# Paged attention of a twelve-sublayer decoder kernel: projections and attention in one program, stacks loaded between the stores, page rows brought by DMA

## The chip, the cores and the metric

The kernel runs on one core of one Trainium2 chip. The metric is the time of one execution on the device, in microseconds (us). The core has five engines that run their own instruction streams and wait for each other by semaphores: TensorE (PE, with its weight loads PEld), VectorE (DVE), ScalarE (ACT), GpSimd (POOL) and SyncE (SP), which issues nearly all DMA transfers of this kernel.

## The reference

The program is a decoder of four layers with three sublayers each (self attention, cross attention, feed-forward), every one wrapped as `x = layernorm(x + f(x))`, on `x` of 2 x 1024 x 256 in fp32. The change concerns the fourth sublayer, the self attention of layer 1. The rest of the reference is left out.

```python
def _L1_attn_ref(x, wq, w_down, wk_up, wv_up, wo):   # N_HEAD = 16, PAGE_SIZE = 64, x: 2 x 1024 x 256
    ...
    q = (x @ wq).reshape(B, T, H, D)
    lat = x @ w_down
    k = (lat @ wk_up).reshape(B, T, H, D)
    v = (lat @ wv_up).reshape(B, T, H, D)
    q = _apply_rope(q, cos, sin)
    k = _apply_rope(k, cos, sin)
    scores = jnp.einsum('bqhd,bkhd->bhqk', q, k) * scale
    pages = jnp.arange(T) // PAGE_SIZE
    allowed = pages[None, :] <= pages[:, None]
    scores = jnp.where(allowed[None, None], scores, jnp.finfo(scores.dtype).min)
    attn = jax.nn.softmax(scores, axis=-1)
    out = jnp.einsum('bhqk,bkhd->bqhd', attn, v).reshape(B, T, E)
    return out @ wo
```

## The kernel before

Every sublayer is a function ("stage") with one or more blocks; in a block each engine has its own program. At the end of each `Mem` its semaphores are cleared and all engines meet at a barrier. In the names of the profile and of the instruction lists the digit of the layer is left out, so `L1_attn_Q` is `L_attn_Q`.

`paged_attention_stage` has two blocks with such a barrier between them.

*The first block* (`L1_attn_qkv`, L186 to L304) makes q, k and v of both batches, in a loop that each engine runs twice (`Fori`). TensorE writes the projections into two PSUM tiles `Y`; VectorE applies the rotary factors (`full`, `rot`, L286 to L292); ScalarE and GpSimd split each result into three bf16 parts whose sum is the fp32 value (`parts`, L261, L300, L263, L303); SP stores the parts to HBM (`parts_dram`, L211). There are four such results in a batch (q in two halves, k in two halves), eight in all; they are called items 0 to 7 here. Each is stored by two transfers. `parts` has two buffers, so the first cast of an item (L261) waits for the stores of the item two before it. At the end SP waits for all stores. The weights and the rotary tables of this block lie in `L_attn_room`, loaded in an earlier stage.

*The second block* (`L1_attn`, from L307) is the attention, in eight rounds of four heads (`it`). For each round SP loads a stack Q and a stack K (`load`, L358 to L363): the parts from HBM, six to a stack and 16 partition rows each, so that one bf16 matmul over the stacked rows gives the product of the fp32 values. Three slots hold the stacks of three rounds. Above the 96 rows of the parts a stack has 8 page rows, which put the mask into the product; above those Q has three rows that SP writes for each round with the negated row maxima (the *neg rows*, L387, three transfers), and K has three rows of ones. A round has a first pass (`row_max`, L407, into `R`; VectorE takes the maxima, L530) and a second pass (scores, L453, into `S`; ScalarE exponentiates, L496; TensorE multiplies by v, L440, into `O`). The first pass of round 0 and twelve of the units of round 1 stand ahead of the second pass of round 0; later, the first pass runs ahead between the second pass's steps. The maxima are split into three bf16 parts on VectorE, turned on TensorE (L415, into `T`), copied by ScalarE (L487) and sent as neg rows; the scores of round 0 wait for them (`neg_in`).

Before the first pass can start, this block sets its constants on VectorE: a memset of `neg`, the ones rows of K in three slots (L518), the identity in bf16 (L519), and from two fp32 tiles `page_q` and `page_k`, which SP loads, the page rows of Q and of K in three slots (L523, L524). TensorE waits for all eleven (`const_set`). SP's order in this block is: output weights `wout`, the 13 transfers for the next sublayer (`following.load`, into `yT`), the page tiles, then the stacks of rounds 0, 1 and 2, and after that the neg rows as the maxima come.

## Time and profile before

| | us |
|---|---|
| runs | 2941.55, 2937.02, 2941.30 |
| median | 2941.3 |
| the profiled execution, its own time | 2937.35 |
| its span, first to last instruction | 2935.5 |
| the stage of the change in it, about | 553 to 960 |

The profile shows one execution. Its times are counted from the start of the span. What lies between the span and the execution's own time is 1.85 us. Busy shares of the whole span average over twelve different stages, so the sections below read the stage itself. "TensorE clock" is the granted clock as a share of 2.4 GHz: 0.50 is 1.2 GHz.

### The profile page before, as it was taken

The page shows a single profiled execution, that of the slowest core. Times are in us where ns is not written, and L with a number is a line of the kernel's source. Part 1 is how long each engine was busy: PE and PEld are TensorE (multiplying, and loading weights), DVE is VectorE, ACT ScalarE, POOL GpSimd, SP SyncE. Part 2 cuts the span into 40 slices and gives each one's busy share as a digit, 9 for nine tenths or more (in the row PEclk, how much of TensorE's full clock was granted, in tenths as well). Part 3 has the DMA queues.
Part 4 walks back from the last instruction along what each step waited for, and adds up shares of the span by engine and source line. Part 5 has one row for each costly group of instructions (what it writes and reads, how often), then busy time and mean ns, then how long its engine had stood idle before and what let it go on. Part 6 is the DMA issues. An engine that isn't in the chain of part 4 may idle for free. (4 is left out here: it accounts for less than half of the span.)

```text
span 2935.5 us, 35285 instructions
## 1 busy us (share of the span) xinstructions
PE 2414.5 (82%) x13995; PEld 1669.9 (57%) x14003; DVE 1503.2 (51%) x2550; ACT 857.4 (29%) x1223; POOL 488.7 (17%) x395
## 2 busy tenths in 40 slices
PE   5876756747888968975999998937999599999888
PEld 3665643422222767763666666735777467777674
DVE  8996966448775340014564565462111345545543
ACT  1111656412556212213433233201111222212132
POOL 3332320130000012311001000102221120000010
PEclk8898978966999979997999999857999799999979
DMA  3002000052441024532322221013222110000000
GB/s 106 0 1 100 2 30 1 11 130 44 67 70 30 13 75 179 212 135 88 92 64 89 61 65 58 8 56 97 96 97 87 68 52 17 17 12 17 1 31 29
DMA packets 71009, 176.71 MB, mean 60 GB/s; under 512 B 16478, under 2 KB 36447, under 8 KB 67280
## 3 DMA queue, kind: packets, MB, share of 16 engines
q1 hardware_dynamic: 60480, 122.60, 15.0%
q0 software_dynamic: 8208, 50.01, 4.8%
q8 instruction: 100, 1.64, 0.2%
q10 hardware_dynamic: 2176, 2.10, 0.2%
q14 instruction: 45, 0.37, 0.0%
HBM read 149.04 MB, written 25.43 MB: 59 GB/s over the span
## 5 line engine op out<-in xcount | busy, mean ns | idle before, releaser
L1575 PE MATMUL L_ffn_h_ps<-L_ffn_xgT,L_ffn_w 128*128 128x512 f32 (+2 forms) x992 | 241.7, 402 | 19.2 <-DMA L_ffn_w<-in_L_ffn_w,group_rows 16.9
L2215 PE MATMUL L_attn_X<-xT,L_attn_w 128*128 128x512 f32 x512 | 227.4, 597 | 0.0
L1587 PE MATMUL L_ffn_y_ps<-L_ffn_w,L_ffn_h 128*128 128x256 f32 x1008 | 223.0, 381 | 4.0 <-ACT L_ffn_h L1612 3.9
L1575 PEld LDWEIGHTS L_ffn_h_ps<-L_ffn_xgT,L_ffn_w 128*128 128x128 f32 x992 | 160.6, 199 | 101.2 <-issue 65.8
L530 DVE TENSOR_REDUCE L_attn_neg<-L_attn_R 128x1 f32<-128x512 f32 (+3 forms) x304 | 187.5, 658 | 54.8 <-PE L_attn_R L407 53.3
L1612 ACT ACTIVATE L_ffn_h<-L_ffn_h_ps,L_ffn_w 128x640 f32<-128x640 f32 (+2 forms) x184 | 101.5, 552 | 388.9 <-PE L_ffn_h_ps L1575 359.1
L1587 PEld LDWEIGHTS L_ffn_y_ps<-L_ffn_w,L_ffn_h 128*128 128x128 f32 x1008 | 190.2, 191 | 32.2 <-ACT L_ffn_h L1612 7.9
L407 PE MATMUL L_attn_R<-L_attn_K,L_attn_Q 104*128 104x512 bf16 (+3 forms) x384 | 119.7, 364 | 83.1 <-DVE L_attn_K L524 48.5
L496 ACT ACTIVATE L_attn_probs<-L_attn_S 128x1024 f32<-128x1024 f32 (+1 forms) x192 | 147.3, 812 | 79.5 <-PE L_attn_S L453 78.9
L2215 PEld LDWEIGHTS L_attn_X<-xT,L_attn_w 128*128 128x128 f32 x512 | 95.2, 191 | 110.1 <-issue 108.3
L1633 DVE COPY L_ffn_xgT<-L_ffn_t_ps 128x256 f32<-128x256 f32 x63 | 24.6, 421 | 246.9 <-PE L_ffn_t_ps L1562 246.9
L1642 DVE TENSOR_TENSOR L_ffn_yg<-L_ffn_y_ps,L_ffn_w 128x256 f32<-128x256 f32 x63 | 26.8, 425 | 227.5 <-PE L_ffn_y_ps L1587 227.5
L2511 PE MATMUL L_attn_X<-xT,L_attn_w 128*128 128x512 f32 x256 | 118.0, 606 | 9.5 <-DMA L_attn_w<-in_L_attn_w 8.9
L407 PEld LDWEIGHTS L_attn_R<-L_attn_K,L_attn_Q 104*128 104x128 bf16 x384 | 33.8, 100 | 157.1 <-DVE L_attn_neg L530 95.2
L1683 POOL DMA_INDIRECT token_outputs<-L_ffn_yg,puts x63 | 61.8, 981 | 366.1 <-DVE L_ffn_yg L1642 366.1
L453 PE MATMUL L_attn_S<-L_attn_Q,L_attn_K 107*128 107x512 bf16 (+3 forms) x384 | 96.3, 337 | 2.0 <-ACT L_attn_probs L496 1.9
L847 POOL TENSOR_TENSOR L_attn_v_all<-L_attn_q,L_attn_kv 128x2048 f32<-128x2048 f32 x16 | 73.9, 4623 | 140.4 <-DVE L_attn_q L780 124.5
L2736 POOL TENSOR_TENSOR L_attn_prod<-L_attn_k_sum,L_attn_qs 128x1024 f32<-128x1024 f32 x16 | 37.7, 2355 | 348.6 <-DVE L_attn_qs L2708 348.6
L2414 POOL TENSOR_TENSOR L_attn_sq_sum<-L_attn_sq_sum,L_attn_sq 128x1024 f32<-128x1024 f32 x14 | 33.0, 2359 | 347.1 <-ACT L_attn_sq L2305 347.1
L2295 ACT ACTIVATE L_attn_bc<-L_attn_bc 128x1024 f32<-128x1024 f32 x32 | 33.8, 1057 | 194.2 <-DVE L_attn_bc L2368 194.2
L440 PE MATMUL L_attn_O<-L_attn_probs,L_attn_v_all 128*32 128x512 f32 (+3 forms) x768 | 82.0, 505 | 0.0
L2511 PEld LDWEIGHTS L_attn_X<-xT,L_attn_w 128*128 128x128 f32 x256 | 48.6, 195 | 58.7 <-issue 57.3
(529 smaller groups left out, 4795.7 us busy)
## 6 DMA issues: line engine op xcount, KB each, us to landing
L_ffn_w<-in_L_ffn_w SPq DMA_DIRECT2D x8, 2180.0 KB
L_attn_bc<-decays SPq DMA_DIRECT2D x32, 512.0 KB, 6.5
L_attn_w<-in_L_attn_w SPq DMA_DIRECT2D x16, 640.0 KB, 3.9
L_attn_bp<-decays SPq DMA_DIRECT2D x32, 256.0 KB, 7.0
L_attn_Q<-L_attn_q_parts SPq DMA_DIRECT2D x48, 128.0 KB, 4.9
L_attn_K<-L_attn_k_parts SPq DMA_DIRECT2D x48, 128.0 KB, 7.4
L_attn_w<-in_L_attn_w SPq DMA_DIRECT2D x16, 384.0 KB, 3.1
token_outputs<-zero SPq DMA_DIRECT2D x1, 4096.0 KB, 20.7
```

Of the source, the lines that this page charges most:

```text
L407: mm = nc.tensor.matmul(R[n % 2][:, u * wdt:(u + 1) * wdt], Q[0:KM, par, j0 + u, tt * P:(tt + 1) * P], K[0:KM, par, j0 + u, c * CW:c * CW ...
L440: mm = nc.tensor.matmul(O[32 * j:32 * j + 32, lo:CW], v_all[:, it, gt, 32 * j:32 * j + 32], probs[:, (2 * n + j // 2) % 4, j % 2, lo:CW], ...
L453: mm = nc.tensor.matmul(S[e % 2][:, j % 2, lo:CW], K[0:KS, par, j, gt * P:(gt + 1) * P], Q[0:KS, par, j, tc * CW + lo:(tc + 1) * CW], star ...
L496: nc.scalar.activation(probs[:, e % 4, :, lo:CW], S[e % 2][:, :, lo:CW], ACT.Exp, scale=SCALE).then_inc(exp_done, 1)
L530: nc.vector.tensor_reduce(neg[:, c, j0:j0 + heads, tt], R[n % 2][:, 0:heads * width(tt, c)].rearrange("p (h k) -> p h k", h=heads), X_AXIS ...
L847: nc.gpsimd.tensor_tensor(prod[n % 2][:, h, :, :], q[n % 2][:, h, :].unsqueeze(2).broadcast_to([P, HALF, H, DH]), keys(n).unsqueeze(1).bro ...
L1575: ins = nc.tensor.matmul(h_ps[f % 2][:, lo // CW, 0:hi - lo], w1[u][:, kt, f * P:(f + 1) * P], xgT[u][:, kt, lo:hi], start=kt == 0, stop=k ...
L1587: ins = nc.tensor.matmul(y_ps[k % 2][:], h[:, f, t * P:(t + 1) * P], w2[u][:, f, :], start=f == 0, stop=f == FT - 1)
L1612: nc.scalar.activation(h[:, f, 0:n], h_ps[f % 2][:].rearrange("p c n -> p (c n)")[:, 0:n], func, bias=b1[g % 2][:, f:f + 1]).then_inc(sem[ ...
L1683: nc.gpsimd.indirect_dma_start(core.outputs, at, yg[g % 2][:, t, :], None).then_inc(y_stored[g % 2], 16)
L2215: ins = nc.tensor.matmul(x[:, c * CW:(c + 1) * CW], w[1 - par][:, kt, r, :], xT[:, kt, b * T + c * CW:b * T + (c + 1) * CW], start=kt == 0 ...
L2511: ins = nc.tensor.matmul(x[:, c * CW:(c + 1) * CW], w[o][:, kt, r, :], xT[:, kt, b * T + c * CW:b * T + (c + 1) * CW], start=kt == 0, stop ...
```

## The change

The two blocks become one, and the barrier between them is gone. Each engine runs its projection program and then, in the same block, its attention program. The loops over the batch are written out. Buffers are shared so that both parts fit: `full`, `rot`, `rest` and `latT` lie in `oT`, `probs` lies in `room` (which holds the projection weights and rotary tables), and `S`, `R`, `O` and `T` are parts of the two PSUM tiles `Y`. New waits keep them apart: TensorE's first maxima wait for `rot_done` of item 6 and for v, its first scores for `rot_done` of item 7, and ScalarE's first copy into `oT` for the last part of item 7.

The page rows and the rows of ones come as bf16 pairs packed into 32-bit words, made on the host and sent by six DMA transfers straight into the stacks, at the very start of the stage. The memsets and casts of VectorE are gone.

SP loads the stacks of rounds 0, 1 and 2 between the stores of the second batch; `wout` and the transfers for the next sublayer follow after the last store. Only loads from round 3 on wait for all stores.

The diff, cut to its core and without the pure re-indentation:

```diff
+    def load(sp, it):
+        par = it % SLOTS
+        for stack, which in ((Q, 0), (K, 1)):
+            for n, part in enumerate(PARTS[which]):
+                src = parts_dram[which][part:part + 1, it:it + 1, :, :].rearrange("c i (j d) t -> (c i d) j t", d=DH)
+                sp.dma_start(stack[n * DH:(n + 1) * DH, par, :, :], src).then_inc(stack_loaded[par], 16)
+
+    oT = m.sb("oT", [P, NI, T])
+    full, rot, rest, latT = oT[:, 0:2, :], oT[:, 2:4, :], oT[:, 4:6, :], oT[:, 6, :]
...
+    def projections_on_sync(sp):
+        for par in range(SLOTS):
+            for stack, rows, src in ((Q, slice(KP, KM), "page_q"), (K, slice(KP, KS), "page_k")):
+                sp.dma_start(stack[rows, par, :, :].rearrange("p j t -> p (j t)").bitcast(I32), A[src]).then_inc(pages_loaded, 16)
+        for b in range(B):
-                with sp.Fori(0, B) as b:
             for r in range(NR):
                 sp.wait_ge(part_done[2], b * NR + r + 1)
                 for g in range(2):
...
+                if b == 1 and r < SLOTS:
+                    sp.wait_ge(stored[r // 2], 16 * NR)
+                    load(sp, r)
-                for par in range(2):
-                    sp.wait_ge(stored[par], 16 * B * NR)
...
-            probs = m.sb("probs", [P, 4, 2, CW])
+        probs = room[:].rearrange("p (u j n) -> p u j n", u=4, j=2)
...
+        S = [Y[1][:, n, :, :] for n in range(2)]
+        R = [Y[0][:, 0, n, :] for n in range(2)]
+        O, Tp = Y[0][:, 1, 0, :], Y[0][:, 1, 1, 0:P]
...
         @block.sync
         def _(sp):
+            projections_on_sync(sp)
             sp.dma_start(wout[:], A[f"{name}_wout"]).then_inc(static_loaded, 16)
             following.load(sp)
-                sp.dma_start(page_q[KP:KM, :], A["page_q"]).then_inc(static_loaded, 16)
-                sp.dma_start(page_k[KP:KM, :], A["page_k"]).then_inc(static_loaded, 16)
...
-                for it in range(SLOTS):
-                    load(it)
...
                         sp.wait_ge(scores_mm, it * NE)
+                        for par in range(2):
+                            sp.wait_ge(stored[par], 16 * B * NR)
+                        load(sp, it + SLOTS - 1)
...
         @block.tensor
         def _(pe):
-                pe.wait_ge(static_loaded, 48)
-                pe.wait_ge(const_set, 11)
+            projections_on_tensor(pe)
+            pe.wait_ge(pages_loaded, 16 * 2 * SLOTS)
+            pe.wait_ge(rot_done, B * NR - 1)
+            pe.wait_ge(v_copied, B)
...
                 pe.wait_ge(neg_in, it * 48 + 48)
+                if it == 0:
+                    pe.wait_ge(rot_done, B * NR)
...
         @block.vector
         def _(dve):
+            projections_on_vector(dve)
             nc.vector.memset(neg[:], 3.0e38).then_inc(const_set, 1)
-                for par in range(SLOTS):
-                    nc.vector.memset(K[KP:KS, par, :, :], 1.0).then_inc(const_set, 1)
             nc.vector.tensor_copy(identb[:], core.ident[:]).then_inc(const_set, 1)
-                dve.wait_ge(static_loaded, 48)
-                dve.wait_ge(const_set, 5)
-                for par in range(SLOTS):
-                    nc.vector.tensor_copy(Q[KP:KM, par, :, :], over(page_q[KP:KM, :], G)).then_inc(const_set, 1)
-                    nc.vector.tensor_copy(K[KP:KM, par, :, :], over(page_k[KP:KM, :], G)).then_inc(const_set, 1)
-                dve.wait_ge(const_set, 11)
+            dve.wait_ge(const_set, 2)
```

How the instructions stand on the two engines that matter most, first on SP. Before, SP's last entries ahead of the neg rows (`L_attn_Q<-L_attn_negT`; the x6 is of rounds 0 and 1) are the end of the transfers for the next sublayer, the page tiles and the stacks of rounds 0 to 2:

```order
L2869 DMA yT<-in_L_xattn_hwf 128x512
L2869 DMA yT<-in_L_xattn_ob 128x256
L355 DMA L_attn_page_q<-in_page_q 8x1024
L356 DMA L_attn_page_k<-in_page_k 8x1024
L363 DMA L_attn_Q<-L_attn_q_parts 16x4x1024 x6
L363 DMA L_attn_K<-L_attn_k_parts 16x4x1024 x6
L363 DMA L_attn_Q<-L_attn_q_parts 16x4x1024 x6
L363 DMA L_attn_K<-L_attn_k_parts 16x4x1024 x6
L363 DMA L_attn_Q<-L_attn_q_parts 16x4x1024 x6
L363 DMA L_attn_K<-L_attn_k_parts 16x4x1024 x6
L387 DMA L_attn_Q<-L_attn_negT 1x32x128 x6
```

In the changed kernel the same stacks stand on SP between the stores of items 4, 5, 6 and 7 (rows with `_parts<-L_attn_parts`), and `wout` follows:

```order
L223 DMA L_attn_q_parts<-L_attn_parts 64x3x1024 x2
L198 DMA L_attn_Q<-L_attn_q_parts 16x4x1024 x6
L198 DMA L_attn_K<-L_attn_k_parts 16x4x1024 x6
L223 DMA L_attn_q_parts<-L_attn_parts 64x3x1024 x2
L198 DMA L_attn_Q<-L_attn_q_parts 16x4x1024 x6
L198 DMA L_attn_K<-L_attn_k_parts 16x4x1024 x6
L223 DMA L_attn_k_parts<-L_attn_parts 64x3x1024 x2
L198 DMA L_attn_Q<-L_attn_q_parts 16x4x1024 x6
L198 DMA L_attn_K<-L_attn_k_parts 16x4x1024 x6
L223 DMA L_attn_k_parts<-L_attn_parts 64x3x1024 x2
L353 DMA L_attn_wout<-in_L_attn_wout 128x1024
```

Behind `wout` come the 13 transfers of the next sublayer, of which these are the last, and then the neg rows:

```order
L2864 DMA yT<-in_L_xattn_ow 128x512
L2864 DMA yT<-in_L_xattn_hwf 128x512
L2864 DMA yT<-in_L_xattn_ob 128x256
L376 DMA L_attn_Q<-L_attn_negT 1x32x128 x6
L198 DMA L_attn_Q<-L_attn_q_parts 16x4x1024 x6
L198 DMA L_attn_K<-L_attn_k_parts 16x4x1024 x6
```

So the transfers of the next sublayer have moved from in front of the stacks to between the stacks and the neg rows.

On VectorE, before, between the end of the projection loop and the first reduction:

```order
L279 COMPARE_AND_BRANCH
L53 UNCONDITIONAL_BRANCH
L514 UNCONDITIONAL_BRANCH
L516 MEMSET L_attn_neg 128x64
L518 MEMSET L_attn_K 11x4096 x3
L519 CAST L_attn_identb<-ident 128x128
L523 CAST L_attn_Q<-L_attn_page_q 8x4096
L524 CAST L_attn_K<-L_attn_page_k 8x4096
L523 CAST L_attn_Q<-L_attn_page_q 8x4096
L524 CAST L_attn_K<-L_attn_page_k 8x4096
L523 CAST L_attn_Q<-L_attn_page_q 8x4096
L524 CAST L_attn_K<-L_attn_page_k 8x4096
```

In the changed kernel, from the rotary work of item 7 to the first reductions (`L_attn_Y` is now the PSUM tile of `R`):

```order
L296 TENSOR_TENSOR L_attn_oT<-L_attn_Y,L_attn_room 128x1024
L298 TENSOR_TENSOR L_attn_oT<-L_attn_Y,L_attn_room 128x1024
L302 TENSOR_TENSOR L_attn_oT<-L_attn_oT 128x1024
L517 MEMSET L_attn_neg 128x64
L518 CAST L_attn_identb<-ident 128x128
L524 TENSOR_REDUCE L_attn_neg<-L_attn_Y 128x4
```

Two of the eleven constants are left on VectorE, and no branch or barrier stands between the two programs.

## Rows read from the trace of the kernel before

**Rows 1.** The page: the span, and part 1, busy time of each engine.
```profile
span 2935.5 us, 35285 instructions
PE 2414.5 (82%) x13995; PEld 1669.9 (57%) x14003; DVE 1503.2 (51%) x2550; ACT 857.4 (29%) x1223; POOL 488.7 (17%) x395
```

**Rows 2.** Windows: busy us of PE, PEld, DVE, ACT, POOL; clock, DMA share, GB/s.
```profile
553.00:642.20 89.20, 59.91 (x144) 28.98 (x144) 30.02 (x24) 22.89 (x27) 34.72 (x16) 0.83 0.29 71
642.20:669.10 26.90, 0.00 (x0) 0.00 (x1) 24.07 (x11) 0.00 (x0) 0.00 (x0) 0.50 1.00 207
669.10:703.30 34.20, 28.41 (x66) 6.25 (x67) 32.04 (x54) 1.54 (x2) 0.00 (x0) 0.50 0.29 48
703.30:960.00 256.70, 223.73 (x1463) 72.54 (x1461) 176.62 (x298) 154.88 (x213) 16.55 (x7) 0.98 0.29 48
```

**Rows 3.** Timeline, 613 to 636 us: start, length, instruction, idle before it.
```profile
613.57 7.03 PE L231 MATMUL L_attn_qkv_Y<-L_attn_qkv_latT,L_attn_room 128*128 128x512 f32 x16
618.51 1.22 DVE L288 TENSOR_TENSOR L_attn_qkv_rot<-L_attn_qkv_Y,L_attn_room 128x1024 f32<-128x1024 f32 x1
626.58 1.23 DVE L292 TENSOR_TENSOR L_attn_qkv_full<-L_attn_qkv_full,L_attn_qkv_rot 128x1024 f32<-128x1024 f32 x1
627.26 2.52 POOL L303 TENSOR_TENSOR L_attn_qkv_parts<-L_attn_qkv_rest,L_attn_qkv_parts 128x1024 bf16<-128x1024 f32 x1 [1.16 <-ACT L_attn_qkv_parts L263]
629.49 1.04 ACT L261 CAST L_attn_qkv_parts<-L_attn_qkv_full 128x1024 bf16<-128x1024 f32 x1 [2.31 <-DMA L_attn_q_parts<-L_attn_qkv_parts]
633.89 2.12 POOL L303 TENSOR_TENSOR L_attn_qkv_parts<-L_attn_qkv_rest,L_attn_qkv_parts 128x1024 bf16<-128x1024 f32 x1 [1.15 <-ACT L_attn_qkv_parts L263]
```

**Rows 4.** Timeline, 642 to 670 us, VectorE and TensorE.
```profile
642.30 0.11 DVE L516 MEMSET L_attn_neg<- 128x64 f32 x1 [14.50 <-PEq L56]
669.13 1.01 PE L407 MATMUL L_attn_R<-L_attn_K,L_attn_Q 104*128 104x128 bf16 x6 [48.53 <-DVE L_attn_K L524]
669.82 25.54 DVE L530 TENSOR_REDUCE L_attn_neg<-L_attn_R 128x4 f32<-128x512 f32 x38 [0.80 <-PE L_attn_R L407]
```

**Rows 5.** Timeline of the DMA queue of SP, 615 to 666 us.
```profile
615.65 9.94 SPq L211 DMA_DIRECT2D L_attn_q_parts<-L_attn_qkv_parts  x4
649.49 2.67 SPq L363 DMA_DIRECT2D L_attn_Q<-L_attn_q_parts  x6
663.44 2.77 SPq L363 DMA_DIRECT2D L_attn_K<-L_attn_k_parts  x6
```

**Rows 6.** The instructions on stack K, 640 to 700 us.
```profile
L363 SPq DMA_DIRECT2D L_attn_K<-L_attn_k_parts x18: 425/426/428, 652.2 to 665.8; - x18
DMA to landing us min/median/max: 6.0/10.1/14.5
```

**Rows 7.** DMA issues, first stack, then third: KB each, median to landing.
```profile
L_attn_K<-L_attn_k_parts SPq DMA_DIRECT2D x6, 128.0 KB, 6.7
L_attn_K<-L_attn_k_parts SPq DMA_DIRECT2D x6, 128.0 KB, 13.5
```

**Rows 8.** Windows: stores of item 4, following weights, three stacks, a later stack.
```profile
616.90:620.40 3.50, 3.50 (x9) 1.33 (x7) 3.40 (x4) 1.04 (x1) 1.79 (x1) 1.00 0.89 221
643.10:651.90 8.80, 0.00 (x0) 0.00 (x0) 6.97 (x3) 0.00 (x0) 0.00 (x0) 0.50 0.96 288
651.90:679.10 27.20, 8.40 (x20) 1.93 (x20) 25.84 (x22) 0.00 (x0) 0.00 (x0) 0.50 1.04 170
771.30:781.80 10.50, 9.45 (x75) 3.56 (x76) 8.32 (x14) 5.71 (x9) 0.00 (x0) 1.00 1.02 142
```

**Rows 9.** Timeline, 699 to 703 us: the neg rows, the first scores.
```profile
699.46 1.89 SPq L387 DMA_DIRECT2D L_attn_Q<-L_attn_negT  x3
703.33 1.06 PE L453 MATMUL L_attn_S<-L_attn_Q,L_attn_K 107*128 107x512 bf16 x2
```

**Rows 10.** Timeline, 759 to 762 us: a cast on VectorE beside GpSimd.
```profile
759.32 2.36 POOL L586 TENSOR_TENSOR L_attn_oT<-L_attn_oT,L_attn_rden 128x1024 f32<-128x1024 f32 x1 [123.31 <-DMA L_attn_rden<-L_attn_inv_dram]
759.34 2.37 DVE L541 CAST L_attn_neg_parts<-L_attn_neg 128x32 bf16<-128x32 f32 x1
```

More of the change, by code:

```diff
@@ L181, in paged_attention_stage @@
     inv_dram = nc.dram_tensor(f"{name}_inv_dram", (G, T), F32, kind="Internal").ap()
[L182 removed]
+    v_all, weights, room, early = early
+    SLOTS = 3
+    PER = 16 * 2 * len(PARTS[0])
     wq = early.tiles["wq"].rearrange("p k (r d) -> p k r d", r=2)
     wk, wv, wdown, cos, sin = [early.tiles[n] for n in ("wk", "wv", "wdown", "cos", "sin")]
[L185 to L591 removed]
@@ L3396, in host_arrays, with halves @@
     own = np.arange(TT)[:, None] == t // P
-    a["page_q"] = np.where(own & (t % P < 64), -1.0e18, 0.0).astype(f)
-    a["page_k"] = np.where(own & (t % P >= 64), 1.0, 0.0).astype(f)
+    def halves(rows):
+        u = np.tile(rows.astype(f), (1, 4)).view(np.uint32)
+        u = (u + 0x7FFF + (u >> 16 & 1)) >> 16
+        return np.ascontiguousarray(u[:, 0::2] | u[:, 1::2] << 16).view(np.int32)
+    a["page_q"] = halves(np.where(own & (t % P < 64), -1.0e18, 0.0))
+    a["page_k"] = halves(np.concatenate([np.where(own & (t % P >= 64), 1.0, 0.0), np.ones((3, T))]))
     d = np.arange(DH)
```

663 lines of the change are left out of this document (320 added, 343 removed).

## The prediction

> **What bounds the kernel now.** The page [rows 1] says only that TensorE is busy for 82% of the span. That is an average over twelve sublayers, and the edit touches one of them, so I went to the windows of that sublayer [rows 2]. The second window is the find: from 642.2 to 669.1 us TensorE runs nothing, VectorE is busy for 24.07 of the 26.9 us with 11 instructions, and the DMA engines are full (share 1.00). Next I read the timeline on both sides of the hole. The last projection matmul starts its run at 613.57 and ends at 620.6; the split of the last part ends on GpSimd at 636.0; VectorE's first instruction of the attention program starts at 642.30 [rows 3, 4]. The first maxima matmul starts at 669.13, and it waited for VectorE's cast of the page rows (L524), 48.5 us of idle in all [rows 4]. So the path through this stage is: projections, last split, barrier at 642.2, eleven constants on VectorE, first maxima. From there VectorE's reductions set the pace (38 of them in 25.54 us without a gap) until the neg rows go out at 699.46 and the scores start at 703.33 [rows 4, 9].
>
> **What is removed.** The barrier with its wait for the last stores: 642.3 - 636.0 = 6.3 us [rows 3, 4]. The three memsets and six casts: nearly all of the 24.07 us that VectorE works before 669.1 [rows 2]. And the order: work that begins after the last split can now begin when its own inputs are there. Unrolling the projection loops changes none of the waits inside them, and I cost it at nothing: before them TensorE's matmuls follow one another without a gap (the run from 613.57 is 7.03 us for 16 [rows 3]), which hides whatever the loop's branches cost or the straight-line code costs to fetch.
>
> **When the first maxima matmul can start now.** It has three conditions; the latest counts.
> First, VectorE's `rot` of item 6: 618.51 + 1.22 = 619.7 [rows 3].
> Second, VectorE itself, which must be free to reduce. Its last projection add ends at 627.8 [rows 3]; then come the memset of neg and the cast of the identity. A cast can be held up by GpSimd: at 759.34 one took 2.37 us and ended together with a GpSimd tensor_tensor that had begun beside it [rows 10]. Here GpSimd works from 627.26 to 629.78 [rows 3], so I put VectorE free at 630.0.
> Third, stack 0. SP issues it after the two stores of item 4 (615.65 [rows 5]). Those stores fill the DMA engines until 620.4 [rows 8]. Behind them stand twelve transfers. In the trace, three stacks take 27.2 us at 170 GB/s with the engines full, so one takes 9.1 us, and the last semaphore comes at 665.8 + 14.5 = 680.3, 1.2 us behind the end of the data at 679.1 [rows 6, 8]. So stack 0 is in at 620.4 + 9.1 + 1.2 = 630.7, and issue doesn't bound it: all 36 issues took from 649.49 to 666.2 [rows 5], 5.6 us for each twelve.
> The stack is last by 0.7 us. The first maxima matmul starts at 630.8 instead of 669.1: **38.3 us** earlier. The cover of VectorE's preparation is thus thin, but being exposed would cost tenths.
>
> **What is late next.** Maxima and reductions take as long as before, since VectorE's reductions set their pace and not TensorE's clock, which is 0.50 in that window now too [rows 2]. So the neg rows are ready 699.46 - 669.13 = 30.3 us after the start, at 661.1. Undisturbed, scores follow 703.33 - 699.46 = 3.9 us later [rows 9], at 665.0. But the three neg transfers are issued on SP, behind everything that SP has issued, and that list has moved too: before, it had emptied by 679.1, twenty microseconds ahead of them [rows 8, 9]. Now, from 620.4 on, the engines have to move, in order of issue: stack 0, stores, stack 1, stores, stack 2, stores, and then the output weights with the thirteen transfers of the next sublayer. That is 3 x 9.1 for stacks, 3 x 3.5 for stores, and 8.8 for the weights [rows 8]: 46.6 us, to 667.0. I checked that the list never runs dry: SP has each next item out before the one ahead of it is done. The last stores depend on a split that now waits for the stores of item 5 queued behind stack 0 (in at about 634.2); it then needs the same 6.5 us as from 629.49 to 636.01 [rows 3], so they go out at 640.7, still ahead of the end of stack 1 at 642.1. The weights follow by 648. The neg rows, issued at 661.1, stand behind them all: data at 667.0, semaphore 1.2 later, scores at about **668.2**. Against 703.33 that is 35.1 us earlier; 3.2 of the 38.3 are handed back.
>
> That a transfer waits for those ahead of it is what the trace shows: the median time to landing of a K transfer grows from 6.7 us in the first stack to 13.5 us in the third, as the backlog grows [rows 7]. The Trainium skill says the same of the mechanism (DMA: Bandwidth & Descriptors, "Queues, rings and completion order"): on each DMA engine the descriptors of one issuing queue are consumed in ring order. By that page the sum is 35.1 us; if small transfers could pass, it would be 38.3 us.
>
> Nothing else is late. Stack 1 is wanted 26 us after the first maxima, at 657, and is in at 643. The page rows go out at the start of the stage, about 60 us ahead of their use. TensorE's wait for `rot` of item 7 and ScalarE's for the last part are over long before the scores start. Behind the delayed split nothing stands but the last stores. The remaining window (703.3 to 960, [rows 2]) holds the same instructions in the same order and moves as a whole, and so do all later sublayers, which start at barriers.
>
> **Sum.** The profiled execution took 2937.35 us (span 2935.5); minus 35.1 gives 2902.3. It lies 3.95 under the median of the three runs, 2941.3, so the forecast on that scale is 2941.3 - 35.1 = **2906.2**.
>
> **Rivals.**
> A, *the neg rows are not held up* (they pass, or the list empties sooner because stores and loads overlap better than one at a time). For it: a store alone reaches 221 GB/s and the weights 288 [rows 8], so mixing may help. Against: the share is already 0.89 to 1.04. It gives the full 38.3: 2903.0, and at most a microsecond more if stack 0 comes sooner, since VectorE is free at 630.0.
> B, *the stacks load slowly.* A later stack, with ScalarE and TensorE at work, went at 142 GB/s, 10.5 us and more [rows 8]; the three (27.2 us at 170 GB/s are 4.62 MB) then take 32.5 us. The list ends at 672.2, the scores start at 673.5, and the gain is 29.8: 2911.5. For it: other engines are now active beside the loads. Against: half the three-stack window had VectorE and TensorE at work and didn't slow.
> C, *the other side: the list in front of the neg rows outlasts the old start.* The place is the same wait. It decides once the list ends past 702.1: after stores and weights (19.3 us) that leaves 62.4 us for the 4.62 MB of stacks, 74 GB/s. At 60 GB/s they take 77.0 us, scores start at 718.0, and the time is 2956.0. Against: the lowest rate in any of these windows is 142.
> D, *nothing is gained*, because the start of the stack loads or of the maxima still hangs on the last store. The order of instructions speaks against it: SP issues stack 0 behind item 4's stores, and only loads from stack 3 on wait for all stores.
>
> **How the numbers follow.** My case (gain 33 to 37) has 0.52, A 0.25, B 0.18, C 0.02, D 0.03. The range reaches from A's 2903.0, less the 4.3 us by which the lowest run of before lies under the median, to B's 2911.5 and 3 more, for the spread of the runs: 2898.5 to 2914.5. The measurement can tell about 0.2%, 5.9 us, from no change; only C and D are not faster than that: faster 0.95, same 0.03, slower 0.02.
>
> **What the new profile would show.** Right: no hole of 48 us before the first maxima matmul; it starts near 631 and its releaser is a stack transfer; VectorE has 25.5 us of reductions without a gap; DMA share near 1 from 617 to about 667; TensorE waits some 3 us before the first scores, released by the neg transfer, whose time to landing is 5 to 7 us instead of two. A shows in a landing near 2 us and scores at 665. B shows as a stack window of 11 us, and the maxima start near 633. It would be wrong by more if VectorE's reductions slowed beside GpSimd's last splits, if the split that waits for item 5's stores came after the queue had run dry, or if a later wait in the stage, now hidden, took the saved time back.

## The result and the profile after

| | us |
|---|---|
| changed kernel, four runs | 2895.08, 2901.28, 2907.30, 2904.22; median 2902.75 |
| kernel before, four runs | 2937.02 to 2944.26; median 2941.43 |
| ratio | 0.9867, 95% interval 0.9842 to 0.9892 |
| the changed kernel once more, five runs beside nine of before | medians 2902.7 and 2943.4; ratio 0.9856, interval 0.9833 to 0.9878 |

The change took 38.7 us off in the first comparison and 40.7 in the second. The forecast was 35.1 (2906.2 for the time), and 2902.75 is inside its range. The interval of the ratio reaches from 32 to 46 us, so the time alone cannot tell the forecast's 35.1 from the 38.3 of rival A. Inside the stage it can be told, and there one step of the forecast did not come true: it came out as rival A had it.

The profiled execution of the changed kernel took 2895.08 us, the fastest of its four, so its whole-span difference (42.2 us) is not the measure. Sublayers that are the same in both kernels differ by a few us between two executions. I therefore count inside the stage, in us from the start of the last projection run: 613.57 before [rows 3], 616.12 after. The page after, span and part 1:

```profile
span 2893.3 us, 35152 instructions
PE 2410.5 (83%) x13995; PEld 1663.4 (57%) x14003; DVE 1480.3 (51%) x2541; ACT 858.1 (30%) x1223; POOL 489.1 (17%) x395
```

The windows that answer to [rows 2]; the columns are the same:

```profile
555.50:642.20 86.70, 68.56 (x169) 31.01 (x168) 41.19 (x41) 23.13 (x27) 34.74 (x16) 0.83 0.46 108
642.20:669.10 26.90, 22.76 (x53) 5.20 (x52) 24.76 (x43) 3.13 (x4) 0.00 (x0) 0.50 0.63 172
631.98:666.16 34.18, 28.41 (x66) 6.32 (x67) 32.56 (x55) 3.63 (x4) 4.59 (x3) 0.50 0.80 216
666.16:921.00 254.84, 221.47 (x1461) 71.73 (x1459) 176.19 (x298) 154.77 (x212) 16.52 (x7) 0.99 0.29 48
```

The hole is gone: in the same 26.9 us TensorE now works 22.76. From the first maxima to the first scores it is 34.18 us, as before (34.20, [rows 2]), with the same 28.41 us of matmuls. The timeline of the changed kernel at the three places that answer to [rows 3, 4, 9]:

```profile
629.13 1.23 DVE L302 TENSOR_TENSOR L_attn_oT<-L_attn_oT 128x1024 f32<-128x1024 f32 x1
630.34 2.07 DVE L518 CAST L_attn_identb<-ident 128x128 bf16<-128x128 f32 x1
631.98 1.01 PE L398 MATMUL L_attn_Y<-L_attn_K,L_attn_Q 104*128 104x128 bf16 x6 [8.83 <-DMA L_attn_K<-L_attn_k_parts]
662.28 1.86 SPq L376 DMA_DIRECT2D L_attn_Q<-L_attn_negT  x3
666.16 1.06 PE L449 MATMUL L_attn_Y<-L_attn_Q,L_attn_K 107*128 107x512 bf16 x2
```

The first maxima matmul waits for a transfer of stack 0, as forecast, and VectorE's cast ends 0.4 us behind its start: the two conditions are nearly even. The scores start 3.9 us after the neg rows are issued, exactly as before [rows 9]. So the neg rows were not held up. From the last projection run on:

| | before | forecast | after | after, second execution |
|---|---|---|---|---|
| first maxima matmul | 55.6 | 17.2 | 15.9 | 16.7 |
| neg rows issued | 85.9 | 47.5 | 46.2 | 47.1 |
| scores | 89.8 | 54.6 | 50.0 | 50.9 |

What became of the list of transfers, in windows of the changed kernel (last two columns: DMA share and GB/s):

```profile
620.00:648.00 28.00, 16.82 (x42) 4.29 (x40) 24.78 (x32) 6.27 (x6) 13.11 (x6) 0.60 1.02 242
648.00:652.00 4.00, 3.34 (x8) 0.64 (x7) 3.78 (x7) 0.00 (x0) 0.00 (x0) 0.50 1.04 316
652.00:660.00 8.00, 6.08 (x16) 1.33 (x16) 7.71 (x16) 0.00 (x0) 0.00 (x0) 0.50 0.82 259
660.00:664.00 4.00, 3.43 (x9) 0.83 (x9) 3.61 (x7) 1.54 (x2) 0.00 (x0) 0.50 0.01 2
```

It is empty by 660, two us before the neg rows go out, where the forecast had it last until 5.9 us after them. The scores are thus 39.8 and 38.9 us earlier than before in the two executions, not 35.1.

### The profile page after: what moved, and what is told of

The parts are those of the page before. It is cut to its first block and busy times, and to the rows that moved or that the text cites. A ratio compares the mean times of both kernels' runs of the same rounds, so it can differ in the third digit from the quotient of the medians.

```text
span 2893.3 us, 35152 instructions
## 1 busy us (share of the span) xinstructions
PE 2410.5 (83%) x13995; PEld 1663.4 (57%) x14003; DVE 1480.3 (51%) x2541; ACT 858.1 (30%) x1223; POOL 489.1 (17%) x395
## 5 line engine op out<-in xcount | busy, mean ns | idle before, releaser
L524 DVE TENSOR_REDUCE L_attn_neg<-L_attn_Y 128x1 f32<-128x512 f32 (+3 forms) x304 | 187.2, 657 | 53.0 <-PE L_attn_Y L398 51.7
L494 ACT ACTIVATE L_attn_room<-L_attn_Y 128x1024 f32<-128x1024 f32 (+1 forms) x192 | 147.2, 812 | 78.3 <-PE L_attn_Y L449 77.7
L398 PE MATMUL L_attn_Y<-L_attn_K,L_attn_Q 104*128 104x512 bf16 (+3 forms) x384 | 118.8, 361 | 43.8 <-DVE L_attn_neg L524 25.9
L398 PEld LDWEIGHTS L_attn_Y<-L_attn_K,L_attn_Q 104*128 104x128 bf16 x384 | 33.5, 99 | 117.3 <-DVE L_attn_neg L524 95.3
L449 PE MATMUL L_attn_Y<-L_attn_Q,L_attn_K 107*128 107x512 bf16 (+3 forms) x384 | 95.4, 334 | 2.0 <-ACT L_attn_room L494 1.9
L434 PE MATMUL L_attn_Y<-L_attn_room,L_attn_v_all 128*32 128x512 f32 (+3 forms) x768 | 81.5, 502 | 0.1
```

The costliest lines, as they stand in the source:

```text
L398: mm = nc.tensor.matmul(R[n % 2][:, u * wdt:(u + 1) * wdt], Q[0:KM, par, j0 + u, tt * P:(tt + 1) * P], K[0:KM, par, j0 + u, c * CW:c * CW ...
L434: mm = nc.tensor.matmul(O[32 * j:32 * j + 32, lo:CW], v_all[:, it, gt, 32 * j:32 * j + 32], probs[:, (2 * n + j // 2) % 4, j % 2, lo:CW], ...
L449: mm = nc.tensor.matmul(S[e % 2][:, j % 2, lo:CW], K[0:KS, par, j, gt * P:(gt + 1) * P], Q[0:KS, par, j, tc * CW + lo:(tc + 1) * CW], star ...
L494: nc.scalar.activation(probs[:, e % 4, :, lo:CW], S[e % 2][:, :, lo:CW], ACT.Exp, scale=SCALE).then_inc(exp_done, 1)
L524: nc.vector.tensor_reduce(neg[:, c, j0:j0 + heads, tt], R[n % 2][:, 0:heads * width(tt, c)].rearrange("p (h k) -> p h k", h=heads), X_AXIS ...
```

## The experiments

Places are in us from the start of the last projection run. Where a run has only one time, its place in the stage is what counts, since single times of one kernel spread over 10 us and more. (These single times are 2924.3 us for experiment 4, 2908.0 for 6, 2892.5 for 7, 2902.2 for 8, 2913.3 for 10 and 2915.0 for 11.) To turn a row's time into a place, subtract the start of that run in the same trace: 616.02 in experiment 1, then 615.89, 615.53, 613.96, 613.64, 615.47, 613.34, 614.45, 613.83, 617.56 and 615.61 in experiments 2 to 11, and 614.05 in the second execution of the changed kernel. Three dots in a diff stand for lines left out.

**1. The page rows alone.** The kernel before, with VectorE's memsets and casts replaced by six transfers.

```diff
+                for par in range(SLOTS):
+                    for stack, rows, src in ((Q, slice(KP, KM), "page_q"), (K, slice(KP, KS), "page_k")):
+                        sp.dma_start(stack[rows, par, :, :].rearrange("p j t -> p (j t)").bitcast(I32), A[src]).then_inc(pages_loaded, 16)
                 sp.dma_start(wout[:], A[f"{name}_wout"]).then_inc(static_loaded, 16)
...
-                for par in range(SLOTS):
-                    nc.vector.memset(K[KP:KS, par, :, :], 1.0).then_inc(const_set, 1)
...
-                    nc.vector.tensor_copy(Q[KP:KM, par, :, :], over(page_q[KP:KM, :], G)).then_inc(const_set, 1)
...
```

> The kernel before with one part of the change alone: page rows and rows of ones come by six DMA transfers at the start of the second block, VectorE keeps only the memset of neg and the cast of the identity. The barrier, the order of the stacks and the separate buffers stay. Theory 1 (VectorE's constants lie over transfers that are just as late): the first maxima matmul then waits for stack 0, which is behind the output weights and the transfers for the next sublayer, and starts at about 663.9 instead of 669.1, released by a stack transfer; time about 5 us less, near 2936. Rival (the constants alone were the hole): it starts near 645, and the time is about 24 us less, near 2917.

2944.7 us beside 2940.3 of before (ratio 1.0014, interval 0.9991 to 1.0037): nothing gained. The first matmul and two windows of this kernel:

```profile
675.41 1.01 PE L407 MATMUL L_attn_R<-L_attn_K,L_attn_Q 104*128 104x128 bf16 x6 [52.36 <-DMA L_attn_K<-L_attn_k_parts]
```
```profile
646.00:652.50 6.50, 0.00 (x0) 0.00 (x0) 0.00 (x0) 0.00 (x0) 0.00 (x0) 0.50 0.96 105
660.00:674.00 14.00, 0.00 (x0) 0.00 (x0) 0.00 (x0) 0.00 (x0) 0.00 (x0) 0.50 1.07 130
```

The releaser is the stack, as theory 1 had it and against the rival: the constants had lain over transfers. But the maxima start at 59.4, 3.8 later than before, not 5 earlier. Two prices were missing from my estimate: 6.5 us at 105 GB/s while the page rows pass, and stacks at 130 GB/s where [rows 8] has 170. With the page rows at the head of SP's list in the second block, the rewritten constants are worth nothing in the old order. Whether some 5 us would be left if the page rows came at another place there was not run.

**2. The constants back on VectorE**, in the changed kernel. The two fp32 page tiles come at the start of the stage, in place of the page rows.

```diff
             nc.vector.memset(neg[:], 3.0e38).then_inc(const_set, 1)
+            for par in range(SLOTS):
+                nc.vector.memset(K[KP:KS, par, :, :], 1.0).then_inc(const_set, 1)
             nc.vector.tensor_copy(identb[:], core.ident[:]).then_inc(const_set, 1)
-            dve.wait_ge(const_set, 2)
...
+            for par in range(SLOTS):
+                nc.vector.tensor_copy(Q[KP:KM, par, :, :], over(page_q[KP:KM, :], G)).then_inc(const_set, 1)
+                nc.vector.tensor_copy(K[KP:KM, par, :, :], over(page_k[KP:KM, :], G)).then_inc(const_set, 1)
+            dve.wait_ge(const_set, 11)
```

> The changed kernel with only the constants put back on VectorE (memsets of the ones rows, six casts from two fp32 page tiles), behind its projection work; no barrier, stacks loaded early. VectorE has some 26 to 27 us of constants from 630.3 on, of which the changed kernel has 2.1. Theory 1: the first maxima matmul starts at 657 to 659 instead of 632.0, released by VectorE; time 25 to 27 us over the changed kernel, near 2929, so 12 to 14 below the kernel before. Rival (with the barrier gone the casts run beside idle engines and cost little): under 10 us over the changed kernel.

2930.2 us (ratio to before 0.9965, interval 0.9945 to 0.9985), 27 over the changed kernel.

```profile
656.87 1.03 PE L398 MATMUL L_attn_Y<-L_attn_K,L_attn_Q 104*128 104x128 bf16 x6 [33.95 <-DVE L_attn_K L525]
```

Maxima at 41.0, 25.1 later, released by VectorE. Theory 1 stands. With the stacks in early, nothing hides the constants: taking them away is worth 25.1 us.

**3. The stacks late again**, in the changed kernel.

```diff
-                    if b == 1 and r < SLOTS:
-                        sp.wait_ge(stored[r // 2], 16 * NR)
-                        load(sp, r)
...
             projections_on_sync(sp)
+            for it in range(SLOTS):
+                load(sp, it)
             sp.dma_start(wout[:], A[f"{name}_wout"]).then_inc(static_loaded, 16)
```

> The changed kernel with only the three stack loads moved behind the stores of item 7, still ahead of the output weights. Theory 1 (early loading of stack 0 is a condition of its own): first maxima at about 653.7 instead of 632.0, released by a stack transfer; time 21 to 22 us over the changed kernel, near 2924.5. The three stacks, no longer among stores, should show again the 170 GB/s that they had alone in the kernel before, against some 250 GB/s of stacks and stores mixed in the changed kernel. Rival (a stack's rate depends on the engines' activity and not on the mix with stores): they keep over 220 GB/s here.

2924.8 us (0.9946, interval 0.9927 to 0.9965), 22 over the changed kernel; the first matmul, and a window in which stacks alone move:

```profile
652.37 1.01 PE L397 MATMUL L_attn_Y<-L_attn_K,L_attn_Q 104*128 104x128 bf16 x6 [29.82 <-DMA L_attn_K<-L_attn_k_parts]
```
```profile
646.00:664.00 18.00, 9.82 (x26) 2.48 (x26) 10.49 (x17) 0.00 (x0) 0.00 (x0) 0.50 1.06 182
```

Maxima at 36.8, 21.0 later, released by the stack: theory 1 for the place. The rate of the stacks alone, 182 GB/s, is near the 170 of [rows 8] and well below the 242 of the mixed stretch after, which speaks against the rival.

**4. Both back at once.** Experiments 2 and 3 in one kernel. What is left of the change is the merging of the two blocks, and that the page tiles and the stacks are issued ahead of the next sublayer's transfers.

> The changed kernel with both of its other parts taken back at once: the constants are VectorE's again, and the three stacks go out behind the stores of item 7. Singly these two moved the first maxima matmul from 15.9 to 41.0 and to 36.8 us after the start of the last projection run (25.1 and 21.0 us). Theory 1 (two conditions of one start, of which the later counts): together 41 again, released by VectorE, not 62; scores at 75, so the second part costs nothing once the first is taken back. Rival (they add up, since the memsets and casts slow the stacks or are slowed by them): over 45.

```profile
654.93 1.04 PE L397 MATMUL L_attn_Y<-L_attn_K,L_attn_Q 104*128 104x128 bf16 x6 [33.94 <-DVE L_attn_K L524]
```
```profile
642.00:662.00 20.00, 5.89 (x16) 1.52 (x16) 18.83 (x16) 0.00 (x0) 0.00 (x0) 0.50 1.06 207
```

Maxima at 41.0, not 62: the later condition counts. The merging alone is thus worth 55.6 - 41.0 = 14.6 us: VectorE's constants begin at 14.2 instead of 28.7 [rows 4], and in both kernels VectorE works them off without waiting for a transfer. The early stacks are worth nothing (41.0 both times) until the constants are gone, and the constants only 41.0 - 36.8 = 4.2 us as long as the stacks are late; together they are worth 25.1. The second row is a surprise: these are the same stack transfers behind the same stores as in experiment 3, and they run at 207 GB/s.

**5. Seven transfers ahead of the neg rows.** Is a transfer held up by what its queue was given before? Seven loads of 512 KB go into a part of `oT` that is not yet in use.

```diff
             following.load(sp)
+            for n in range(7):
+                sp.dma_start(oT[:, 1 + n, :], A["x_tok"].rearrange("p s d -> p (s d)")[:, n % 4 * T:(n % 4 + 1) * T]).then_inc(filled, 16)
...
```

> The changed kernel with seven more transfers of 512 KB from an input into a part of oT that is not in use yet, issued on SP behind the transfers for the next sublayer and ahead of the neg rows of round 0 (what they bring is overwritten later). In the changed kernel the list was empty at 659.6, before the neg rows went out at 662.3. Theory 1 (a transfer stands behind what its queue was given before): the list now ends near 672, the neg rows land some 9 us after their issue instead of 1.9, the scores start at about 673.5, 7 us later than in the changed kernel, and the time is up by as much, near 2910. Rival (small transfers pass large ones): neg rows land in about 2 us, scores at 666, no change of the time.

2910.4 us, the median of five (ratio to before 0.9913, interval 0.9886 to 0.9941). SP's queue, then TensorE, then two windows of this kernel, and from issue to landing of its neg rows:

```profile
654.28 4.39 SPq L357 DMA_DIRECT2D L_attn_oT<-in_x_tok  x7
660.44 1.86 SPq L379 DMA_DIRECT2D L_attn_Q<-L_attn_negT  x3
670.32 1.03 PE L452 MATMUL L_attn_Y<-L_attn_Q,L_attn_K 107*128 107x512 bf16 x2 [5.80 <-DMA L_attn_Q<-L_attn_negT]
```
```profile
664.00:666.00 2.00, 0.52 (x1) 0.01 (x1) 1.23 (x2) 0.00 (x0) 0.00 (x0) 0.50 1.01 412
666.00:668.00 2.00, 0.00 (x0) 0.00 (x0) 0.00 (x0) 0.00 (x0) 0.00 (x0) 0.50 0.48 167
```
```profile
DMA to landing us min/median/max: 7.0/7.1/8.6
```

The neg rows, issued at 660.4 while the engines were full, landed only after the list had run out near 667: 7.0 to 8.6 us after issue, instead of 1.8 to 1.9. The scores came 9.9 us after the issue instead of 3.9, at 56.7, 6.6 later than in the changed kernel (expected 7). So a neg row does wait for what the same queue was given before it, as the forecast's last step has it; in the changed kernel nothing was left in front of it.

**6. The same seven behind the neg rows.**

```diff
                                  negT[G * TT * c:G * TT * (c + 1), :]).then_inc(neg_in, 16)
+                if it == 0:
+                    for n in range(7):
+                        sp.dma_start(oT[:, 1 + n, :], A["x_tok"].rearrange("p s d -> p (s d)")[:, n % 4 * T:(n % 4 + 1) * T]).then_inc(filled, 16)
...
```

> The changed kernel with the same seven 512 KB transfers as in the run with seven ahead of the neg rows, but issued right behind the neg rows of round 0. It separates the place in the queue from the mere load on the DMA engines. Theory 1 (the queue's order): neg rows land in about 2 us again, scores start 50.0 us after the last projection run begins, no loss in the stage (under 0.5 us). Rival (more bytes in flight slow whatever is near): scores later by over 1 us.

```profile
663.33 1.87 SPq L377 DMA_DIRECT2D L_attn_Q<-L_attn_negT  x3
665.24 3.90 SPq L381 DMA_DIRECT2D L_attn_oT<-in_x_tok  x7
```

Landing in 1.9 us and scores 3.9 after issue: the same bytes behind the neg rows cost nothing. The seven had hardly begun to move when the neg rows landed, though, so how neg rows fare beside full engines on a queue of their own was not tried. The scores stand at 51.7, not 50.0, because stack 0 came 1.7 us later, long before the seven were issued; the expectation missed that scatter of the stack's landing (first maxima at 15.9, 16.5, 16.7 and 17.6 in four executions with the same list up to there).

**7. Stack 0 earlier.** SP issues stack 0 ahead of item 4's stores, stacks 1 and 2 behind those of items 4 and 5.

```diff
             for b in range(B):
                 for r in range(NR):
+                    if b == 1 and r == 0:
+                        sp.wait_ge(stored[0], 16 * NR)
+                        load(sp, 0)
                     sp.wait_ge(part_done[2], b * NR + r + 1)
...
-                    if b == 1 and r < SLOTS:
-                        sp.wait_ge(stored[r // 2], 16 * NR)
-                        load(sp, r)
+                    if b == 1 and r < 2:
+                        sp.wait_ge(stored[r], 16 * NR)
+                        load(sp, r + 1)
```

> The changed kernel with each stack issued one store pair earlier: stack 0 ahead of the stores of item 4, stacks 1 and 2 behind the stores of items 4 and 5. It separates the two conditions of the first maxima matmul. Theory 1 (VectorE, held in the cast of the identity by GpSimd until about 632.4, is as late as stack 0 within 0.5 us): stack 0 lands 5 us earlier or more, but the first reduction moves by less than 0.5 us; the matmul itself may start earlier, the scores stay within 0.5 us of 50.0 after the last projection run begins. Rival (only the stack holds it): scores 3 us earlier or more.

```profile
627.57 2.07 DVE L520 CAST L_attn_identb<-ident 128x128 bf16<-128x128 f32 x1
629.67 4.39 DVE L526 TENSOR_REDUCE L_attn_neg<-L_attn_Y 128x4 f32<-128x512 f32 x7
```

The first maxima matmul now starts at 6.9, but the first reduction only at 16.3 (16.6 in the changed kernel), and the scores at 49.8. VectorE was the second condition, as late as the first within a few tenths. It is held in the cast of the identity, which takes 2.07 us here beside GpSimd's split of item 6; where it runs later, with GpSimd idle (experiment 4), it takes 0.23.

**8. And the constants earlier**, on top of 7. Memset and cast stand ahead of VectorE's projection work.

```diff
-            projections_on_vector(dve)
             nc.vector.memset(neg[:], 3.0e38).then_inc(const_set, 1)
             nc.vector.tensor_copy(identb[:], core.ident[:]).then_inc(const_set, 1)
+            projections_on_vector(dve)
```

> The kernel with stack 0 early, and VectorE's memset of neg and cast of the identity moved ahead of its projection work, where VectorE waits anyway. With both conditions moved, the first reduction should start when VectorE's last projection add ends, about 14.5 us after the start of the last projection run instead of 16.6: scores 2.1 us earlier, 47.9. If the gain is under 0.5 us, a third condition holds the maxima, and the releaser of the first maxima matmul or of the first reduction names it.

```profile
628.60 5.78 DVE L526 TENSOR_REDUCE L_attn_neg<-L_attn_Y 128x4 f32<-128x512 f32 x9
```

First reduction at 14.2, scores at 47.6 (expected 47.9): with both conditions moved, 2.4 us are gained, with the stack's alone 0.2. The constants' alone was not run.

**9. Three maxima in VectorE's gap**, on top of 8; ahead of item 7's rotary work VectorE waits 2.3 us for GpSimd.

```diff
+                    if n == B * NR - 1:
+                        for u in range(3):
+                            maximum(0, u)
...
-            for n in range(NU):
+            for n in range(3, NU):
                 maximum(0, n)
```

> The kernel with stack 0 and the two constants early, and besides VectorE reduces the first three maxima units in its 2.3 us wait ahead of the rotary work of item 7, where it waits for GpSimd anyway. Theory 1 (from the first reduction on only VectorE's work counts, so work put into its gap is gained whole): scores 45.5 us after the start of the last projection run begins, 4.5 before the changed kernel, neg rows at 41.6; time 4 to 5 us under the changed kernel. The list of transfers is empty near 654 in the kernels with early stacks, so neg rows sent at about 657 still find it empty. Rival (the three reductions end after GpSimd's piece and delay the rotary work and with it the rest): 47.6 or later.

```profile
622.00 1.88 DVE L528 TENSOR_REDUCE L_attn_neg<-L_attn_Y 128x4 f32<-128x512 f32 x3
624.38 1.23 DVE L301 TENSOR_TENSOR L_attn_oT<-L_attn_Y,L_attn_room 128x1024 f32<-128x1024 f32 x1 [0.50 <-POOL L_attn_parts L317]
627.98 2.17 DVE L528 TENSOR_REDUCE L_attn_neg<-L_attn_Y 128x1 f32<-128x384 f32 x4
```

Scores at 45.6 as expected, 4.4 and 5.3 ahead of the two executions of the changed kernel, and its neg rows found the list empty. The time is 2900.4 us (ratio to before 0.9847, interval 0.9828 to 0.9865) against 2902.7 of the changed kernel on the same chip: lower by 2.3 where 4 to 5 were expected, and these runs, spread over 9 and 14 us, can't tell it from zero. The stage's gain is shown, a shorter whole is not.

**10. The page rows at another place.** The six transfers move from the start of the stage to right ahead of stack 0.

```diff
-            for par in range(SLOTS):
-                for stack, rows, src in ((Q, slice(KP, KM), "page_q"), (K, slice(KP, KS), "page_k")):
-                    sp.dma_start(stack[rows, par, :, :].rearrange("p j t -> p (j t)").bitcast(I32), A[src]).then_inc(pages_loaded, 16)
             for b in range(B):
...
+                    if b == 1 and r == 0:
+                        for par in range(SLOTS):
...
                     if b == 1 and r < SLOTS:
                         sp.wait_ge(stored[r // 2], 16 * NR)
                         load(sp, r)
```

> The changed kernel with only the six page-row transfers moved from the start of the stage to right ahead of stack 0 on SP. In the changed kernel they occupy the DMA engines for 5 to 6 us from 558 on (0.47 MB in 57 packets of 8 KB), beside idle engines. Theory 1 (that is their price wherever they stand, and at the start of the stage nothing hears of it): the first maxima matmul starts 4 to 6 us later, 20 to 22 us after the start of the last projection run instead of 15.9. Theory 2 (they also slow the stacks behind them, as the 132 GB/s of the kernel with the page rows alone suggests): the stacks run below 180 GB/s as well and the maxima start 8 us later or more. Rival (their bytes are few, so they hide among stores and stacks): under 2 us.

```profile
642.08 1.01 PE L399 MATMUL L_attn_Y<-L_attn_K,L_attn_Q 104*128 104x128 bf16 x6 [17.49 <-DMA L_attn_K<-L_attn_k_parts]
```
```profile
632.00:638.00 6.00, 0.00 (x0) 0.00 (x0) 1.86 (x1) 0.00 (x0) 1.78 (x1) 0.50 1.07 148
656.00:662.00 6.00, 5.07 (x11) 0.95 (x10) 5.82 (x10) 0.00 (x0) 0.00 (x0) 0.50 1.05 154
```

Maxima at 24.5, 8.7 later: theory 2. The stacks run at about 150 GB/s even 30 us behind the page rows. At the start of the stage no cost of the same transfers shows: from the stage's first matmul to the last projection run it takes 58.9 us before and 58.6 after.

**11. The same, in short packets.** Each row of 8 KB is laid out in memory as four pieces. The diff is against experiment 10.

```diff
-                    sp.dma_start(stack[rows, par, :, :].rearrange("p j t -> p (j t)").bitcast(I32), A[src]).then_inc(pages_loaded, 16)
+                    sp.dma_start(stack[rows, par, :, :].rearrange("p j t -> p (j t)").bitcast(I32).rearrange("p (s t) -> p s t", s=4),
+                                 A[src].rearrange("(s p) t -> p s t", s=4)).then_inc(pages_loaded, 16)
...
```

> The kernel with the page rows ahead of stack 0, with one thing altered: each row of 8 KB lies in memory as four pieces of 2 KB, so that the same 0.47 MB come in 228 packets of 2 KB instead of 57 of 8 KB. It tells apart why the stacks behind them ran at 140 to 157 GB/s instead of 180 and more. Theory 1 (57 long packets do not divide evenly over 16 DMA engines and leave them out of step): with four times as many short ones the stacks are back at 180 or more, and the first maxima matmul starts 18 to 21 us after the start of the last projection run instead of 24.5. Theory 2 (their place counts, few partition rows written beside the stacks, whatever the packets): 140 to 157 again, and the maxima stay at 23 or later.

```profile
639.13 1.01 PE L400 MATMUL L_attn_Y<-L_attn_K,L_attn_Q 104*128 104x128 bf16 x6 [16.49 <-DMA L_attn_K<-L_attn_k_parts]
```
```profile
622.00:630.00 8.00, 0.64 (x2) 0.00 (x0) 5.60 (x6) 3.13 (x3) 5.69 (x4) 0.68 0.94 124
642.00:646.00 4.00, 3.55 (x7) 0.70 (x7) 3.71 (x7) 1.11 (x2) 2.71 (x2) 0.50 1.06 173
```

Neither theory holds whole. The later stacks are at 173 to 185 GB/s again, but the maxima start at 23.5, only 1.0 sooner: while the page rows pass, the rate is still 124 GB/s. So the stacks behind ran faster with the short packets, in one execution of each kernel; why the page rows themselves pass slowly stays open.

## Why the forecast was right, and which step failed

- *The hole, and what is removed.* Right. Experiments 2 and 4 show the parts: 14.6 us for the merging and 25.1 for constants and early stacks together, 39.7 in all; without the early stacks the constants are worth 4.2.
- *Start of the first maxima.* Forecast 17.2 after the last projection run, measured 15.9 and 16.7. VectorE was put free 16.4 after it; its cast ended at 16.3. Stack 0 was in 1.4 us and 0.5 us sooner than 9.1 us at 170 GB/s gave. "The stack is last by 0.7 us" holds in kind: experiments 7 and 8 show two conditions within a few tenths. That "issue doesn't bound it" rested on 5.6 us for twelve issues; here the twelve of stack 0 took 8.1 us (619.2 to 627.4), and no run shows whether that held the stack back.
- *Maxima to neg rows.* Forecast 30.3, measured 30.3.
- *The hand-back of 3.2 us.* Wrong. The step that failed is the term "46.6 us, to 667.0", the list of transfers summed at the rates that each kind had alone. In the frame of after it should have run from 622.9 to 669.5; it ended near 660. Some 37 us took the place of 46.6. That the neg rows would wait for such a list is right (experiment 5), its length is not, so rival A came true by its second reason, "the list empties sooner", and not by its first, "they pass". The gain in the stage, 39.8 and 38.9 us, lies outside the 33 to 37 of the forecast's own case. That the time fell inside the range is due to the range's reaching to rival A, and that it lies only 3.5 us from the forecast is partly luck: runs of one kernel spread over 12 us. (By its own terms the range begins at 2903.0 - 4.3 = 2898.7, not at 2898.5.)
- *The terms inside it.* Three stacks (4.7 MB) and three pairs of stores (2.4 MB) were put at 37.8 us; at the 242 GB/s of 620 to 648 they take 29. Two things are in this. Where the next stores join a stack, the rate is far above either alone: 392 GB/s in a window of 2 us of the second execution, where the stack alone had 171 just before.

```profile
626.00:628.00 2.00, 0.00 (x0) 0.00 (x0) 1.90 (x2) 1.04 (x1) 0.84 (x2) 0.50 1.08 171
630.00:632.00 2.00, 1.01 (x6) 0.56 (x6) 0.86 (x2) 0.00 (x0) 0.27 (x1) 0.50 1.09 392
```

  And the stacks alone have no fixed rate: 170 before, 182 in experiment 3, 207 in 4, 130 in 1. I can't divide the nine us between the two.
- *"The list never runs dry."* The forecast had the last weights issued by 648, which is 650.5 in the frame of after. SP issued without a pause from 618 on and needed until 657:

```profile
656.56 0.43 SPq L2864 DMA_DIRECT2D yT<-in_L_xattn_ob  x1
```

  From 652 to 660 the DMA engines were busy for only 0.82 of the time. The 36 stack transfers landed 3.3 to 5.3 us after issue, where before it was up to 14.5 [rows 6]: SP's issues and the engines kept step, and no backlog grew in front of the neg rows. Which of the two set the pace, no run separates.
- *Nothing else is late.* Right as far as the runs tell. From the scores to the output projection it took 257.7 us before and 256.1 and 258.6 in the two executions after; that scatter is also where a microsecond or two of experiment 9 may have gone, and no run here settles it.

That each DMA engine takes the descriptors of one queue in ring order is also what the Trainium skill states (DMA: Bandwidth & Descriptors, "Queues, rings and completion order"). Experiment 5 agrees, with 7.0 to 8.6 us from issue to landing against 1.9.

## What to carry to other kernels

When one start has several conditions, take away each and all: here the rewritten constants alone gave nothing in the old order and 4.2 us behind the merging, the early stacks without them nothing, and together 25 us on top of the merging. A sum of transfer times at solo rates came out a quarter too long here, for a list in which loads and stores alternate; before charging a wait to the end of such a list, see by how much the end may move, and put the decisive small transfer ahead of whatever is not urgent. The transfers to a handful of partition rows cost 8.7 us in front of a stack that was waited for, and nothing visible where the DMA engines were idle; that is where such transfers belong.

## What the runs showed of the hardware

- Transfers to few partition rows were slow, and the busy share of the DMA engines doesn't tell it. Six page-row transfers (8 and 11 rows of 8 KB, 0.47 MB) took some 6 us at the start of the stage, and in experiment 1 the windows with them read 105 GB/s at a share of 0.96. Lists of transfers to 16 rows ran at 130 to 207 GB/s at shares of 1.04 to 1.07, beside 333 at 1.04 for the 128-row weights of experiment 3:

```profile
668.50:674.50 6.00, 5.09 (x11) 0.97 (x10) 5.68 (x11) 0.00 (x0) 0.00 (x0) 0.50 1.04 333
```

  The Trainium skill (SBUF — State Buffer, "Door 1: The DMA port swizzle") makes the rate a matter of how many of 16 ports the partitions reach; by its figures partitions 0 to 15 reach four ports, about 109 GB/s for one transfer. The lists here ran above that, so by that page transfers must have overlapped. No run here shows the ports, so that they set the rate is argued and not shown, and it leaves open why one list ran at 182 in experiment 3 and at 207 in 4.
- SP's issue was slower right behind a pair of large stores. Six stack issues took 2.67 us before [rows 5] and 4.93 us behind the stores of item 4 in the changed kernel, with the six after them back near 3:

```profile
617.96 1.23 SPq L223 DMA_DIRECT2D L_attn_q_parts<-L_attn_parts  x2
619.24 4.93 SPq L198 DMA_DIRECT2D L_attn_Q<-L_attn_q_parts  x6
624.21 3.15 SPq L198 DMA_DIRECT2D L_attn_K<-L_attn_k_parts  x6
```

  The issue for stack 0 thus ended at 627.4, 4.6 us before the first maxima matmul. Stores are not the only place: in experiment 1 the last six stack issues, behind thirty others and no store, took 5.13 us. What slows them stays open.

```profile
668.84 5.13 SPq L363 DMA_DIRECT2D L_attn_K<-L_attn_k_parts  x6
```
